# Weighted one-hot rows of a graph gather made on VectorE alone, one instruction per gather, between the adds

## The reference, cut to what matters

```python
def _L0_gnn_ref(x, edge_row, edge_col, edge_val, weight, bias):
    support = x @ weight
    msgs = edge_val[:, None] * support[edge_col]
    agg = jax.ops.segment_sum(msgs, edge_row, num_segments=N_NODES)
    return jax.nn.relu(agg + bias + x)

xn = _layernorm(x, axis=-1)
x = x + _L0_gnn_ref(xn, src, dst, edge_weight, L0_gnn_weight, L0_gnn_bias) + _L0_mix_ref(xn[None], ...)[0]
x = x + _L0_ffn_ref(_layernorm(x, axis=-1)[None], ...)[0]
```

## Time and profile before

| | us |
|---|---|
| median of 3 runs (lowest to highest) | 3411.77 (3410.58 to 3417.18) |
| the profiled execution's own time | 3419.82 |
| its span from first to last instruction | 3418.1 |

### The profile page before, as it was taken

The page is one execution under the profiler, slowest core; times in us unless marked ns, Lnnn a source line. Parts: engine busy times, 40 slices in busy tenths (PEclk is TensorE's granted clock), DMA queues, the critical chain, the costliest instruction groups (busy, mean ns, idle before and its releaser), DMA issues.

```text
span 3418.1 us, 41727 instructions
## 1 busy us (share of the span) xinstructions
PE 2595.2 (76%) x10366; PEld 1964.0 (57%) x10366; DVE 2142.3 (63%) x4967; ACT 1244.5 (36%) x2686; POOL 2204.1 (64%) x2119
## 2 busy tenths in 40 slices
PE   5898887677777786687687687687687657888886
PEld 2777776545545454555465455455455536777775
DVE  7999999645555657657656666665766664544311
ACT  0111111044444444343343344344343414444432
POOL 1455554577777777777777777777777744555533
PEclk8666666579889888898998898899899867999998
DMA  3111113155453544544444444444444374544445
GB/s 133 34 35 37 39 35 96 19 128 123 119 123 114 116 117 119 124 118 126 121 116 127 117 116 127 116 117 128 116 113 116 119 253 119 116 114 106 97 78 118
DMA packets 418835, 368.04 MB, mean 108 GB/s; under 512 B 252024, under 2 KB 357024, under 8 KB 418368
## 3 DMA queue, kind: packets, MB, share of 16 engines
q0 software_dynamic: 106752, 249.84, 27.8%
q1 hardware_dynamic: 303376, 106.10, 13.3%
q10 hardware_dynamic: 8496, 9.75, 0.8%
HBM read 293.12 MB, written 72.24 MB: 107 GB/s over the span
## 4 chain that ended last, share of the span: by engine, by line
PE 29%; DVE 23%; issue 10%; DVEq 8%; POOL 7%; DMA 3%; ACT 1%; SPq 0%; POOLq 0%; ACTq 0%
DVE R L1555 11%; PE ps L930 8%; DVEq L1546 6%; PE ps L1004 5%; PE ps L996 4%; PE ps L1119 4%; POOL rows L768 3%; PE ps L1107 2%; POOL routed L790 2%; POOL total L811 2%; DVEq L1555 1%; DVE is_low L1542 1%; PE ps L964 1%; DVE xnT L1615 1%; PE ps L947 1%
## 5 line engine op out<-in xcount | busy, mean ns | idle before, releaser
L768 POOL DMA_INDIRECT rows<-support,t_dst x1624 | 1593.2, 981 | 498.8 <-issue 463.3
L930 PE MATMUL ps<-rows,hot 128*128 128x256 f32 x3248 | 915.8, 435 | 382.9 <-DVE R L1555 328.5
L1555 DVE TENSOR_TENSOR R<-R,ps 128x256 f32 x1624 | 683.3, 421 | 725.9 <-PE ps L930 283.5
L930 PEld LDWEIGHTS ps<-rows,hot 128*128 128x128 f32 x3248 | 684.3, 219 | 608.0 <-issue 309.8
L1231 ACT ACTIVATE hot<-is_low,t_w 128x128 f32<-128x128 bf16 x1624 | 689.4, 513 | 185.9 <-DVE is_low L1542 133.7
L742 POOL DMA_INDIRECT slots<-rec,st_pos x224 | 308.8, 1378 | 354.9 <-issue 169.0
L874 PE MATMUL ps<-spread,piece 128*104 128x96 bf16 x1568 | 305.9, 372 | 47.1 <-DVE spread L1464 47.0
L811 POOL DMA_INDIRECT total<-y_w,zt x112 | 176.8, 1578 | 248.1 <-DVE y_w L1878 211.8
L874 PEld LDWEIGHTS ps<-spread,piece 128*104 128x104 bf16 x1568 | 301.7, 286 | 57.8 <-DVE spread L1464 38.3
L1119 PE MATMUL ps<-w_all,h_t 128*128 x896 | 221.7, 405 | 1.9 <-DVE y_w L1878 1.9
L1875 DVE TENSOR_TENSOR y_w<-ps,b_b 128x512 f32<-128x512 f32 x56 | 38.7, 692 | 276.7 <-PE ps L1119 246.3
(11 more groups left out here) (261 smaller groups left out, 2914.9 us busy)
## 6 DMA issues: line engine op xcount, KB each, us to landing
rows<-support,t_dst POOLq DMA_INDIRECT x1624, 2.8
zt<-routed SPq DMA_DIRECT2D x56, 268.0 KB, 3.1
xa<-in_x SPq DMA_DIRECT2D x24, 512.0 KB
w_all<-in_L_ffn_W SPq DMA_DIRECT2D x16, 512.0 KB, 10.6
R<-zeros SPq DMA_DIRECT2D x1, 6400.0 KB, 27.4
out<-total SPq DMA_DIRECT2D x1, 6250.0 KB, 22.5
xin<-in_x SPq DMA_DIRECT2D x12, 512.0 KB
support<-sup_sb ACTq DMA_DIRECT2D x12, 512.0 KB
```

What stands on the lines that cost most here:

```text
L768: pool.indirect_dma_start(out=rows[h][:, j, :], out_offset=None, in_=support, in_offset=bass.IndirectOffsetOnAxis(ap=t_dst[a][:, col:col + ...
L930: last = pe.matmul(ps[q][:, t * D:(t + 1) * D], lhsT=hot[o][:, q * 2 + t, :], rhs=rows[h][:, q * 2 + t, :], start=True, stop=True)
L1555: dve.tensor_tensor(out=there, in0=there, in1=ps[q][:, t * D:(t + 1) * D], op=ALU.add).then_inc(carried, 1)
```

## The change

The joint comparison (`select`, `is_low`, `iota_x`) and ScalarE's copies (`weigh_edges`) are removed. `point(s, k)` makes the 128 x 128 `hot` of one gather in one VectorE instruction: it compares the row 0..127 (`iota_row`, float32) with the gather's column of `t_low` and multiplies by its column of `t_w`, both read per partition. `carry_on(s)` now issues after each of its eight adds one `point` of step s + 2; steps 0 and 1 are made before the loop. `t_low` becomes float32, `convert` waits on `summed` in place of `hot_done`, and GpSimd's `iota_x` before the gather goes. A filler, `apart`, is enlarged so that the buffers allocated after it keep their places.

```diff
--- before.py
+++ after.py
@@ -65,7 +65,6 @@
 ROWS = 4
 HOTS = 3
 AHEAD_HOT = HOTS - 1
-AHEAD_LOW = AHEAD_HOT + 1
 WIN = 8
 NWIN = -(-STEPS_G // WIN)
 NPART = 4
@@ -287,14 +286,12 @@
         dest_i = alloc(early, "dest_i", [P, NG], I32)
         raws = [alloc(early, f"raws{a}", [P, WT, RECW], BF16) for a in range(2)]
         t_dst = [alloc(early, f"t_dst{a}", [P, WT], I32) for a in range(2)]
-        t_low = [alloc(early, f"t_low{a}", [P, WT], BF16) for a in range(2)]
+        t_low = [alloc(early, f"t_low{a}", [P, WT]) for a in range(2)]
         t_w = [alloc(early, f"t_w{a}", [P, WT]) for a in range(2)]
         rows = [alloc(early, f"rows{h}", [P, HALF, D]) for h in range(ROWS)]
         hot = [alloc(early, f"hot{h}", [P, HALF, P]) for h in range(HOTS)]
-        is_low = [alloc(early, f"is_low{h}", [P, P, HALF], BF16) for h in range(2)]
-        iota_x = alloc(early, "iota_x", [P, P, HALF], BF16)
         nought = alloc(early, "nought", [P, 2 * (P + 4)])
-        apart = alloc(early, "apart", [P, 368 - E * HC])
+        apart = alloc(early, "apart", [P, 1840 - E * HC])
         xa = alloc(early, "xa", [P, GB, D])
         xf = alloc(early, "xf", [P, GB, D])
         xn = alloc(early, "xn", [P, GB, D])
@@ -416,7 +413,6 @@
         xa_in = sem("xa_in")
         xf_in = sem("xf_in")
         conv_done = sem("conv_done")
-        is_low_done = sem("is_low_done")
         hot_done = sem("hot_done")
         kxn_done = sem("kxn_done")
         ktr_done = sem("ktr_done")
@@ -754,7 +750,6 @@
                 pool.wait_ge(scattered[s], SCAT_ALL)
             pool.wait_ge(sup_stored, STORES)
             pool.memset(nought[:, :], 0.0)
-            pool.iota(iota_x[:, :, :], [[1, P], [0, HALF]], base=0, channel_multiplier=0, allow_small_or_imprecise_dtypes=True)
             pool.iota(iota_g, [[1, NG]], base=0, channel_multiplier=0, allow_small_or_imprecise_dtypes=True).then_inc(iota_done, 1)
 
             for s in range(STEPS_G):
@@ -1220,17 +1215,6 @@
             pack(NQ - 1, 1)
 
 
-            def weigh_edges(s):
-                a, h, o = s // WIN % 2, s % 2, s % HOTS
-                act.wait_ge(is_low_done, s + 1)
-                act.wait_ge(conv_done, s // WIN + 1)
-                if s >= HOTS:
-                    act.wait_ge(summed, (s - HOTS + 1) * UNITS)
-                for k in range(HALF):
-                    col = s % WIN * HALF + k
-                    last = act.activation(hot[o][:, k, :], is_low[h][:, :, k], ACT.Copy, scale=t_w[a][:, col:col + 1])
-                last.then_inc(hot_done, 1)
-
             def keys(b):
                 if b >= 2:
                     act.wait_ge(acc_done, b - 1)
@@ -1240,11 +1224,7 @@
                 act.activation(krelu[:, b % 2, :], kraw[:, b % 2, :], ACT.Relu).then_inc(kexp_done, 1)
 
             copy_transposed(0, GB, (4, 5), ktr_done, xnT, ktrc_done)
-            for s in range(AHEAD_HOT):
-                weigh_edges(s)
             for s in range(STEPS_G):
-                if s + AHEAD_HOT < STEPS_G:
-                    weigh_edges(s + AHEAD_HOT)
                 for b in kv_at(s):
                     keys(b)
                     if b % GB == GB - 1:
@@ -1526,7 +1506,7 @@
                 flat = raws[a][:, 0:n, :]
                 dve.wait_ge(raw_in[a], w // 2 * 16 + 16)
                 if w >= 2:
-                    dve.wait_ge(hot_done, (w - 1) * WIN)
+                    dve.wait_ge(summed, (w - 1) * WIN * UNITS)
                 seq(dve.tensor_tensor(out=t_w[a][:, 0:n], in0=flat[:, :, 3], in1=flat[:, :, 4], op=ALU.add))
                 dve.tensor_tensor(out=t_w[a][:, 0:n], in0=t_w[a][:, 0:n], in1=flat[:, :, 5], op=ALU.add)
                 dve.tensor_copy(out=t_low[a][:, 0:n], in_=flat[:, :, 2])
@@ -1534,13 +1514,16 @@
                                              op0=ALU.mult, op1=ALU.add))
                 dve.sem_inc(conv_done, 1)
 
-            def select(s):
-                a, h = s // WIN % 2, s % 2
-                if s >= 2:
-                    dve.wait_ge(hot_done, s - 1)
-                col = s % WIN * HALF
-                dve.tensor_tensor(out=is_low[h][:, :, :], in0=iota_x[:, :, :],
-                                  in1=t_low[a][:, None, col:col + HALF].to_broadcast([P, P, HALF]), op=ALU.is_equal).then_inc(is_low_done, 1)
+            def point(s, k):
+                a, o, col = s // WIN % 2, s % HOTS, s % WIN * HALF + k
+                if k == 0 and s % WIN == 0:
+                    dve.wait_ge(conv_done, s // WIN + 1)
+                if k == 0 and s >= HOTS:
+                    dve.wait_ge(summed, (s - HOTS + 1) * UNITS)
+                last = dve.tensor_scalar(out=hot[o][:, k, :], in0=iota_row[:, :], scalar1=t_low[a][:, col:col + 1],
+                                         scalar2=t_w[a][:, col:col + 1], op0=ALU.is_equal, op1=ALU.mult)
+                if k == HALF - 1:
+                    last.then_inc(hot_done, 1)
 
             def carry_on(s):
                 _, where = nc.values_load_multi_w_load_instructions(dest_i[0:1, s * HALF:(s + 1) * HALF], [mybir.EngineType.DVE], min_val=0, max_val=NB)
@@ -1553,6 +1536,8 @@
                         if t == 0:
                             dve.wait_ge(summed, s * UNITS + q + 1)
                         dve.tensor_tensor(out=there, in0=there, in1=ps[q][:, t * D:(t + 1) * D], op=ALU.add).then_inc(carried, 1)
+                        if s + AHEAD_HOT < STEPS_G:
+                            point(s + AHEAD_HOT, q * 2 + t)
 
             def widen_keys(g):
                 dve.wait_ge(xa_in, g * 16 + 16)
@@ -1646,8 +1631,8 @@
             dve.wait_ge(sup_stored, STORES)
             convert(0)
             dve.wait_ge(iota_done, 1)
-            select(0)
-            select(1)
+            for k in range(HALF):
+                point(0, k)
             dve.tensor_scalar(out=gflags[0:NB, :], in0=iota_g[0:NB, :], scalar1=gcol[0:NB, 0:1],
                               scalar2=None, op0=ALU.is_ge).then_inc(flags_done, 1)
             dve.memset(vaug[:, :, :, P:P + 1], 1.0)
@@ -1659,10 +1644,9 @@
             last.then_inc(dest_done, 1)
             dve.wait_ge(dest_done, 1)
             dve.wait_ge(r_zero, 16)
-            select(2)
+            for k in range(HALF):
+                point(1, k)
             for s in range(STEPS_G):
-                if s + AHEAD_LOW < STEPS_G:
-                    select(s + AHEAD_LOW)
                 carry_on(s)
                 if s % WIN == 1 and s // WIN + 1 < NWIN:
                     convert(s // WIN + 1)
```

## The result

The change makes the kernel slower by 0.9%. The median of six runs is 3444.2 us (3440.7 to 3445.9) against 3413.3 us (3405.6 to 3417.2) for the kernel before on the same chip; the ratio is 1.0089, with a 95% interval of 1.0078 to 1.0100. The profiled execution took 3440.7 us, and its span of 3439.0 us is 20.9 us longer than that of before. The medians are 30.9 us apart. The mean granted clock of TensorE is 0.827 in both.

What follows compares the result with a forecast made beforehand. GpSimd's gather issue was taken as the bound by a hair, TensorE and VectorE next; 38 + 5 - 4.5 - 7.5 = +31 us on the profiled 3419.8 gave 3451, stated as 3442 for a median; range 3398 to 3465.

Steps and rivals of the forecast that it cites:

- the pair: TensorE and VectorE, which hand each other PSUM banks; said to be slower than GpSimd from about 1245 us on.
- A `point`: Duration of one point instruction on VectorE: 0.35 us, with bounds 0.30 and 0.36.
- Add and point, 0.605 us: VectorE's adds: with a point behind each, one add and point take 0.605 us, against 0.564 per add before.
- 0.55 us per step in which VectorE leads: Loss per VectorE-led step: 0.29 us until the last add plus 0.265 behind it; bounds 0.20 and 0.7.
- 3.7 us a period: Loss per 12-step period: 7 x 0.55 - 0.4 + 0.25; over 10.2 periods +38 us for the pair.
- +5 from the key part: First 42 steps: 23 us of VectorE delay, mostly swallowed by TensorE's waits for gathers; +5 us left.
- -4.5 of relief for the gathers: Gathers freed of collisions with `is_low`, 19 us over the stage; a quarter, before the pair takes over, comes off.
- rival B: Port sharing on GpSimd: each point holds up gathers it meets, 80 us less 19, giving 3473 us; chance 0.10.
- -7.5 in hand: GpSimd's buffers of `rows`: 6 gathers of 1.26 us still in hand at the end absorb 7.5 us of delay.
- after 2590 the backlog melts and the gathers set the pace again: End of the gather stage: gathers lead again after 2590 us, and its small terms cancel.
- Rival A: The pair gets no slower, GpSimd stays the bound and loses its collisions: 3397 us; chance 0.20.
- Rival C: In between: a step costs 0.2 us, a period 1.25, +3 us in all, giving 3415 us; chance 0.13.

Runs made afterwards that it cites:

- e11: The changed kernel with every point in the loop issued twice, the second into a scratch buffer nobody reads: 3744.9 us, ratio 1.0956 to the kernel before.
- e12: The kernel before with three buffers of gathered rows in place of four: 3419.7 us, ratio 1.0006 to the kernel before.
- e1: The changed kernel with the eight points issued ahead of the register reads, not between the adds, on a slower chip: 3851.6 us, ratio 1.0034 to before.
- e8: The kernel before, unchanged, run again for its trace on a slower chip: 3830.2 us, ratio 1.0000.

## Why the prediction was right, point by point

The forecast case happened by its own mechanism: the pair gets slower, its delay fills the buffers of `rows`, and GpSimd stands still. The time (3442) is 2 us from the median (3444.2), and that closeness is in part luck. The sum, +31 us, was worked out from traces, and by the traces the difference is 20.9 us; only the medians are 30.9 apart. Term by term: the pair lost 29.8 us where 38 + 5 = 43 was forecast, the 4.5 of relief for the gathers did not reach the end, and the 7.5 in hand came out near (7.1) because two misses cancel.

- **A `point`.** 0.35 us forecast, median 0.345 measured, within 0.30 and 0.36. Right.
- **Add and point, 0.605 us.** 0.587 measured in the median of the key steps (4.11 / 7). The mechanism is right: a point starts 0.34 us behind the add, as work without a wait did before, and the next add starts 0.26 (not 0.265) behind the point.
- **0.55 us per step in which VectorE leads.** 0.42 measured on both kinds of chip (9.29 against 8.87). This was the mis-sized term. The part up to the last add is 7 x 0.023 = 0.16 us and not 0.29, for the eight adds before lay 0.564 apart and now 0.587; the part behind it is 0.26 as forecast. The second point of `e11`, which finds no gap, costs 2.05 us a step, five times as much: most of the first point lies in the time that an add waits for its forerunner.
- **3.7 us a period.** 27.4 us over the ten periods from step 54 to 174, 2.7 each, so 28 over the 10.2 of the sum and not 38; it ends at 24.6 behind, and the steps up to 198, for which the forecast had nothing, add 5.2. The shortest step behind the reciprocal is 0.13 us shorter than before (9.29 against 9.42): `is_low` can give back more than the points take there, as forecast, though the median of the 24 steps with a reciprocal is 0.18 longer than before (10.77 against 10.59). The 0.25 for the handing over of quarters can't be told apart.
- **+5 from the key part.** At step 42 the adds are 8.7 us late, at step 54 they are 2.8 early. TensorE's waits for landed gathers swallowed all of it, more than forecast; in the stretch of the earlier trace rows they are gone from the longest ten.
- **-4.5 of relief for the gathers.** 3.9 us at step 114. The share given to `is_low`, 19 us, is right: in the trace of before the 104 gathers with an `is_low` running 0.13 us after their start last 1132 ns on average, 18.6 us over the usual 953 ns in all. But the gather time fell by 1593.2 - 1581.8 = 11.4 us only, since the points have collisions of their own (6.4 us, under rival B). And none of it comes off the end, which in the kernel after is not set by the gathers.
- **-7.5 in hand.** It shows where forecast: GpSimd idles from 1903 us on. There was more of it: `e12` says about 10 us, and at the end the adds of step 198 are 29.8 late and the last gather 17.9, so the buffers took 11.9 off. But the step "after 2590 the backlog melts and the gathers set the pace again" failed. Gathers set the pace at the end of before; in the kernel after the backlog has not melted by the last gather, and the last add is 4.8 us later still. So it is 29.8 - 11.9 + 4.8 = 22.7 at the end of the gather, and that 11.9 - 4.8 is close to 7.5 is luck.
- **From there to the span** it is 20.9 us, so 1.8 us come back in the third stage. That stage, from the last add to the end, takes 642.1 us in the trace of before, 640.3 after, 638.8 in `e12` and 642.0 in `e11`, so this much is scatter. The medians say 30.9, with an interval of 27 to 34. Where the medians' further 8 to 10 us lie can't be read from any trace.
- **Rival A** needed the pair to lose less than 0.7 us a period; it lost 2.7. **Rival B** needed gathers above 1.0 us; they fell to 974 ns. The 848 gathers that overlap a point in the trace of after last 6.4 us in all over 953 ns each, the doubled points add 9.0 us, and against the kernel without points it is 5 to 15 us, where B had 80. The Trainium skill, "SBUF — State Buffer", "Who interferes with whom", lets a tensor_scalar in a two-port mode that issues first hold the shared ports for its whole length. If the points are such instructions, the trace does not agree: 407 gathers have a point running 0.13 us after their start, and held until its end they would have lost 79 us; they lost 5.4. **Rival C** had 1.25 us a period. One more was raised with the experiments, a `hot` that comes late at TensorE: in the trace of after TensorE waits for it four times, 1.0 us in all, where before it waited 43 times for ScalarE's, 140.2 us.
- **The chain** of one period after (2145 to 2273), against the earlier trace rows:

```profile
by line: PE ps L925 15.6%; issue 12.7%; DVE R L1538 12.5%; PE ps L991 10.7%; PE ps L999 10.3%; DVEq L1529 10.0%; DVE hot L1523 6.4%; PE ps L959 2.7%; DVE xnT L1600 2.4%; DVE stats L1450 2.1%; DVE qneg L1616 1.3%; DVE fin L1616 1.3%; DVE qph
```

  Adds and points together have 18.9% where the adds alone had 19.3: the chain now runs through a point where it ran through the end of an add. The comparison's 2.3% is gone.
- **What should show in the profile:** eight adds and points in 4.9 us (4.8: 2056.57 + 0.35 - 2052.12), backlog at 32 past 2000 us (29 at 2017.5, blocks from 1903 on), idle times ended by TensorE of 20 to 35 us beyond the old 0.31 (70.3 - 135 x 0.305 = 29): right. ScalarE's busy time fell from 1244.5 to 569.0, by 676 (689 forecast). VectorE's rose by 170, not 430: the page counts time in which it is busy, and an add and its point cover 0.587 us, not 0.417 + 0.357. The sum of their durations did rise by 578 - 138 = 440.

That the cost is made by the points' place between the adds is shown by the undisturbed steps of three kernels (8.88 without, 8.90 with them ahead of the reads, 9.29 between). That it sets the whole time on a chip of the first kind is shown by the doubled points and by the waits, not by taking them out: the kernel without points did not run on such a chip. On the slower chips the change costs at most 0.35% by its interval; why they are slower, and why it costs less there, is open.

## What to carry to other kernels

Work put between dependent instructions is not priced by its duration but by the gap that is there: the first 0.35 us point cost 0.05 us per add, the second, in the same place, 0.26. Look also at what an engine's sequencer does, which no busy time shows: reading eight register values took longer than eight points (in `e1` the adds wait 0.58 us more behind the points' 2.13), and points put there cost 0.03 us in the usual step, while the bounds test on them was worth more (1.3 to 1.6%, on the slower chips) than the change could lose. And follow a delay to the last instruction of its stage: here it had grown to 29.8 us in the adds, and 7.1 us came back, because the old kernel itself waited for its gathers at the end. Last, a sum of differences read from one trace of each kernel is to be held against traces: two medians can lie 10 us further apart than the two executions that were profiled.

## What the runs showed of the hardware that was not expected

- Single Trainium2 chips differ by 12% on this kernel: before took 3412 to 3419 us on two and 3811 to 3836 us on four others, with the same durations of its instructions (adds 421 ns on both) and much more idle time between them. The mean granted clock was 0.827 on the first and 0.782 in `e8`.
- A change of 0.9% on one kind was 0.1% (not told from none) on the other, and doubling the points, 9.6%, was run only on the first. Which chip a comparison runs on decided what it could see.
- A 0.34 us VectorE instruction that reads SBUF and writes 128 x 128 float32 was nearly free for GpSimd's indirect DMAs beside it (5 to 15 us in 1624), while the bfloat16 comparison of 0.68 us, a tensor_tensor with both inputs in SBUF, could stretch a gather from 0.95 to 1.37 us and cost 18.6 us in 104 gathers.
- Eight adds that each wait for the one before them start 0.564 us apart though they last 0.42, and one independent 0.345 us instruction between them makes it only 0.587; a second makes it 0.844.
- Reading eight block numbers into registers takes VectorE's sequencer 2.85 us (0.61 for the load at 1020.39 us of before, then 0.28 for each tested value), and none of it counts as busy.
